# Three matmuls on constant weights ahead of each half's second feed-forward layer, in a one-core hybrid transformer block

## The reference, cut to what matters

```python
x = x + attn_a(layernorm(x))    # 16 heads of 8, softmax over 1024 keys
x = x + ffn(layernorm(x))
x = x + attn_b(layernorm(x))    # 8 heads, the nearest 32 of a window of 64, then a decoder
x = x + ffn(layernorm(x))

def ffn(x):                     # weights are +1 or -1
    h = s0 * (concat([x, -x]) @ w0)     # 256 -> 512
    h = s1 * ((relu(h) * 2) @ w1)       # 512 -> 512: the layer of the change
    return s2 * ((relu(h) * 2) @ w2)    # 512 -> 128
```

## Time and profile before

| | |
|---|---|
| median of three runs (lowest, highest) | 2771.61 us (2760.75, 2773.98) |
| the profiled execution, its own time | 2766.34 us |
| its span, first to last instruction | 2764.6 us |
| mean granted TensorE clock | 0.907 of full speed |
| busy: PE, ACT, DVE, POOL | 86%, 78%, 77%, 20% of the span |
| matmuls of the second layer (hparts,W) | 992 of 1024 under this name, 310.2 us busy |

### The profile page before, as it was taken

One profiled execution on the slowest core, in us unless ns is written; L12 is line 12 of the kernel. 1 busy time (PEld: TensorE's weight loads), 2 busy tenths in 40 slices (PEclk: granted clock), 3 DMA queues, 4 the chain that ended last, 5 costly groups with the idle time before them and its releaser, 6 DMA issues.

```text
span 2764.6 us, 62837 instructions
## 1 busy us (share of the span) xinstructions
PE 2381.7 (86%) x22227; PEld 1037.3 (38%) x22227; DVE 2120.0 (77%) x10307; ACT 2161.5 (78%) x2935; POOL 559.5 (20%) x744
## 2 busy tenths in 40 slices
PE   3788788998899888999899898999899888997766
PEld 1111343344332543335432453335433454235444
DVE  4910769977798778987799777987799877992684
ACT  3799678988699777987789777997779876994443
POOL 3020013212141113211141111412132120111241
PEclk6599698999899998999899998999999998998777
DMA  3111000110011001110001100110001100000000
GB/s 88 37 44 42 11 24 18 52 47 10 24 52 50 19 7 27 57 55 9 24 30 45 47 6 24 58 52 11 19 16 59 52 10 16 12 19 1 19 21 12
DMA packets 98525, 84.92 MB, mean 31 GB/s; under 512 B 19954, under 2 KB 79540, under 8 KB 98212
## 3 DMA queue, kind: packets, MB, share of 16 engines
q1 hardware_dynamic: 97968, 80.41, 9.8%
q10 hardware_dynamic: 244, 0.49, 0.1%
HBM read 55.32 MB, written 25.44 MB: 29 GB/s over the span
## 4 chain that ended last, share of the span: by engine, by line
PE 45%; ACT 31%; DVE 16%; issue 6%; SPq 2%; POOL 1%; DMA 0%; ACTq 0%; DVEq 0%; POOLq 0%
PE banks L909 41%; ACT PT L1268 17%; ACT pq L1255 3%; DVE xn L1623 3%; DVE h L1626 3%; DVE pq L1397 2%; PE banks L916 2%; ACT h L1276 1%; ACT hparts L1275 1%; ACT xn L1208 1%; ACT h L1334 1%; ACT h L1337 1%; ACT h L1176 1%; SPq L621 1%; DVE B L1581 1%
## 5 line engine op out<-in xcount | busy, mean ns | idle before, releaser
L1268 ACT ACTIVATE PT<-banks 128x1024 f32<-128x1024 f32 x1024 | 988.8, 1029 | 46.0 <-PE banks L909 40.8
L1397 DVE CUSTOM_DVE_ANT_0 pq<-pq,banks 128x512 f32<-128x512 f32 x1024 | 650.6, 683 | 138.1 <-ACT pq L1255 134.8
L1255 ACT ACTIVATE pq<-banks 128x1024 f32<-128x1024 f32 x512 | 523.6, 1023 | 241.6 <-PE banks L909 214.3
L909 PE MATMUL banks<-PT,Vg 128*9 128x512 f32 x4096 | 546.5, 607 | 6.3 <-ACT PT L1268 6.2
L909 PE MATMUL banks<-K,Q 48*128 48x512 bf16 x2048 | 372.5, 439 | 104.9 <-ACT pq L1255 52.4
L909 PE MATMUL banks<-Q,K 51*128 51x512 bf16 x2048 | 385.0, 396 | 77.7 <-ACT PT L1268 59.3
L1623 DVE MATCH_REPLACE8 xn<-h,xn 128x96 f32<-128x96 f32 x1536 | 352.0, 241 | 0.0
L909 PE MATMUL banks<-hparts,W 128*128 128x512 f32 x992 | 310.2, 452 | 18.7 <-ACT h L1276 6.2
L909 PEld LDWEIGHTS banks<-Q,K 51*128 51x128 bf16 x2048 | 92.2, 93 | 567.6 <-ACT PT L1268 464.9
L859 POOL TENSOR_TENSOR hparts<-h,hparts 128x512 fp32r<-128x512 f32 x108 | 136.1, 1278 | 657.0 <-ACT h L1276 657.0
L1626 DVE MAX8 h<-xn 128x8 f32<-128x96 f32 x1536 | 262.7, 243 | 0.0
(11 more groups left out here) (227 smaller groups left out, 3253.2 us busy)
## 6 DMA issues: line engine op xcount, KB each, us to landing
Vw<-scratch_v SPq DMA_DIRECT2D x256, 51.0 KB, 1.9
scratch_k<-pq SPq DMA_DIRECT2D x24, 384.0 KB, 3.0
K<-scratch_k SPq DMA_DIRECT2D x126, 72.0 KB
qkf<-in_hidden_states SPq DMA_DIRECT2D x16, 512.0 KB, 4.9
scratch_q<-pq SPq DMA_DIRECT2D x24, 256.0 KB, 2.1
Q<-scratch_q SPq DMA_DIRECT2D x126, 48.0 KB
K<-scratch_k SPq DMA_DIRECT2D x126, 48.0 KB
scratch_v<-Bs SPq DMA_DIRECT2D x8, 544.0 KB, 3.6
```

The source lines that it names most:

```text
L909: return pe.matmul(o, l, r, start=start, stop=stop)
L1255: act.activation(cut(g), ring_pair if work is TURN0 and g % 2 else pair[0], ACT.Relu).then_inc(diff_out.sem, 1)
L1268: act.activation(PT[:, at:at + 2, :], pair[g % ESLOTS], ACT.Exp, scale=1.0 if i % 8 < 4 else -1.0).then_inc(probs.sem, 1)
L1397: dve.tensor_tensor_reduce(r, r, pair[1 + g % 2][:, par, :], 1.0, -3.0e38, ALU.subtract, ALU.max, mred[:, par, i, qt:qt + 1]).then_inc(max ...
```

## The change

On PE alone, in front of the first matmul of every half's second layer, the wait for the ring bank comes first, then three matmuls of 128 x 128 weights and 512 columns are issued into that bank (both operands are parts of the constant W1), and only then the wait for the fourth `fa`'s eviction. Nothing reads what they leave: the layer's own first matmul starts the bank anew. The waits themselves are the same ones, in another order. No other engine's stream is touched.

```diff
+            def busy(bank, times):
+
+                for _ in range(times):
+                    mm(bank[:, 0:HALF], W1[:, 0, 0:P], W1[:, 1, 0:HALF], True, True)
+
...
                         if f == 0:
+                            pe.wait_ge(*R.free(c, k))
                             if o == 0:
+                                busy(R.bank(k), 3)
                                 pe.wait_ge(*R.made(c, k, use["fa", (n, 2)], use["fa", (n, 3)]))
-                            pe.wait_ge(*R.free(c, k))
                         if o == 0:
                             pe.wait_ge(*(low_p if side == "p" else low_q).at(b, FC * (n % 2) + f + 1))
```

## The result

The changed kernel takes 2771.32 us (median of 20 runs, 2764.30 to 2779.11), the kernel before 2765.76 us in the runs beside it (20 runs, 2760.01 to 2777.12). The ratio is 1.0019, with a 95% interval from 1.0010 to 1.0028. That is slower by 5.2 us (0.19%): within the 0.5% that the prediction called "same" and inside its range of 2755 to 2781 us, but clear of zero, where the forecast had gain and costs cancel.

The account below looks back on a forecast made before the run. PE's matmuls were taken to bound the kernel, slowed by half-clock stretches after short idle gaps. -14.3 + 4.2 + 2.8 + 4.5 + 2.9 = +0.1 us on 2766.34; forecast 2767 us, range 2755 to 2781.

Parts of the forecast that it names:

- Half (3): Turns 2 to 7: added matmuls fill 1.04 us of PE idle time, half-clock stretches go; -14.3 us.
- there is nothing to give the loss back: From half (3)'s third layer to the next half (3), the chain was taken as no shorter after a long half (3).
- signs of being wrong: Half-clock stretches remaining at half (3), turns shorter than turn 5's by more than the added matmuls, or new low stretches.
- Half (1): Turns 1 to 7, clock low in all: no gain, added matmuls cost their own time; +4.5 us.
- the trio starts when the layer would have, and merely stands in for it: At half (1), the reason given for expecting no gain from the three added matmuls, within the +4.5 us.
- Half (2): Turns 2 to 7: no PE idle time before the layer, so 0.7 us each goes on the path; +4.2 us.
- half (0): Turns 1 to 7: hidden by 1.18 us idle at full clock, 0.7 us in four low-clock turns; +2.8 us.
- Tail: Six places after the turns: costs at (0), (1), (4) and (5), none at (2) and (3); +2.9 us.
- Rival 1: Half-clock stretches stay at half (3), or move by a few us and take the same; 2781 us, chance 0.15.
- Rival 2: At (0) and (1), 14 places cost 1.3 us each, and half (3)'s half-clock stretches stay; 2792 us, chance 0.08.
- Rival 3: Costs at (2), (0) and (1) hide behind ACT and DVE, only the tail's 2.9 remain; 2755 us, chance 0.13.
- The rule named against the change: Clock drops come from longer PE-idle gaps, so filling 1 us gaps at half (3) saves nothing and only costs stay.

Follow-up runs that it names:

- half3_narrow: Changed kernel with added matmuls only at half (3) of turns 2 to 7, each of 8 columns instead of 512; 0.9997 of the kernel before.
- half3_only: Changed kernel with the three added matmuls only at half (3) of turns 2 to 7; 0.9973 of the kernel before, 7.4 us faster.
- early1: As half3_only, plus three matmuls per turn ahead of the wait of the K,Q pair before half (1)'s layer; 0.9962 of the kernel before.
- tail_only: Changed kernel with added matmuls only at the six places of the tail; 0.9992 of the kernel before.
- not_half3: Changed kernel with added matmuls at the 26 other places, none at half (3) of turns 2 to 7; 1.0059 of the kernel before, 16 us slower.
- early_both: As half3_only, plus three matmuls ahead of each of three waiting K,Q pairs per turn, one before half (1)'s layer, two behind; 0.9916 of the kernel before.
- early_ln: As half3_only, plus three matmuls ahead of each of two K,Q pairs about 22 us behind half (1); 0.9895 of the kernel before, 2738.91 us.
- half3_half1: Changed kernel with added matmuls only at half (3) and half (1), outside the tail; 0.9999 of the kernel before.
- early_narrow: As early_both, but the early added matmuls stream 8 columns instead of 512, those at half (3) whole; 0.9964 of the kernel before.

## Why the prediction was wrong

**Half (3), forecast -14.3.** The mechanism at the place was right: the trio fits the idle 1.04 us, the falls of turns 2, 4, 6 and 7 are gone, that of turn 3 is shorter (and turn 5 has a short one that it had not), and half3_narrow shows that it is the clock. The figure was right for the place (-12.6 in the changed trace, -13.9 in half3_only) and wrong for the kernel: 7.4 us. This is the step that failed, and the term that the sum had wrong: "there is nothing to give the loss back". It was read from the distance between one half (3) and the next, 302.0 and 300.5 us, as if that distance were fixed. The two distances quoted stand behind turns 2 and 5, whose halves (3) are the shortest, so they do not bear on long ones; behind turns 3, 4 and 6 it is 302.2, 303.6 and 300.0 us, not shorter either. But it is not fixed: it contains falls of its own, which come or stay away, and with the trios in place more of them came behind half (1) (24.2 us over the least in half3_only, 10.9 to 22.3 without wide trios). The reading of turn 7 was slightly off, too: 2239.05 - 2221.54 is 17.51 and not 17.44, which leaves the sum as it is. Two of the prediction's own signs of being wrong are in the changed trace: a fall remains at (3) in turn 3, and new ones stand where there were none, as in turn 6 above.

**Half (1), forecast +4.5.** Too small as well. Its seven trios cost 11.6 us alone and 7.2 beside half (3)'s, where the places show 3.6 to 5.8. The sentence "the trio starts when the layer would have, and merely stands in for it" held, and early1 shows what the place is worth: in front of a wait as many matmuls cost nothing.

**Half (2), +4.2, and half (0), +2.8.** The places cost 3.1 and 1.5 in the changed trace; alone the trios cost 6.6 and 5.5 us, with intervals of 4 us to either side. The cover at (0), 1.18 us of idle time, was there and held at full clock.

**Tail, +2.9.** 3.9 in the changed trace, but tail_only gives -2 us with an interval that takes in zero. The costs at (0) and (1) are there; in its trace they are made up for further on.

**The sum.** Two runs split it. Everything but half (3) (not_half3) cost 0.59%, 16 us, against a forecast of 14.4, which lies inside its interval. Half (3) alone gained 0.27%, 7.4 us, against 14.3, which does not. So the miss of the sum is half (3)'s: its whole local gain was taken, and half of that did not reach the end. Added, the two runs give +0.32%, uncertain by 0.17%; the whole change measures +0.19%. Trios outside half (3) may cost less when half (3) is covered (0.46% against 0.59%), but that difference is within the noise. The five places taken alone add up to -0.27 + 0.42 + 0.24 + 0.20 - 0.08 = +0.51%, uncertain by 0.3%, so that the parts don't add is not shown either.

**The rivals.** Rival 1 (falls stay, or move by a few us and take the same) is wrong for the place: the falls there went or got shorter. But about half of the gain was lost again, and the traces have more falls about 50 us behind half (1), which the rival did not name. Rival 2 priced the trios at (0) and (1) at 18.2 us; alone they cost 5.5 + 11.6 = 17.1. That is near by luck: the seven places of each cost 2.8 and 3.6 us by the account, not the 7 x 1.3 = 9.1 of its mechanism, and the rival's other half, that falls stay at (3), did not come. Rival 3 (the costs hide) holds at (0) where the clock is full, and in the tail's sum by tail_only. Its condition, trios in idle time that ACT sets, is what early_both and early_ln then built.

**The rule named against the change.** The section "Why this matters for your kernels" of the Trainium skill's "TensorE: Matmul & The Clock Gate" lays drops to long idle gaps between bursts. Here trios into stretches of 1.04, 0.96 and 0.78 us took falls away: those at (3) alone won 7 us, all of them together 29. By that rule they would have won nothing, and the measurement decides.

**What stays open.** Why half of what half (3) gains is lost again is not known. Falls behind half (1) come with trios at any of the four halves, so a shift in the time of what follows may be the cause as well as the missing falls at (3); no run moved the work without adding matmuls. No trio was tried in the low stretch of 13.7 us at the change from the maxima to the softmax (740.0 to 753.7 in turn 2 of the kernel before, clock 0.50).

## What to carry to other kernels

Filler matmuls paid here in front of a wait that PE had anyway, into a bank that was free before that wait; behind the wait the same filler cost its own time and more (early1 0.9962 against half3_half1 0.9999). Look for all short idle stretches that a fall of the clock follows, not for the one that was noticed first: the early trios behind half (1) brought the time from half3_only's 0.9973 to 0.9916 (early_both) and 0.9895 (early_ln), two to three times what the trio at half (3) had won. And where falls come and go between executions of one kernel, a gain read at one place is not the kernel's: time each place alone, in many runs, before adding them up.

## What was unexpected in the hardware

The clock falls with no idle stretch in front. Before `sq,own` in turn 6 of the changed kernel PE went from one matmul to the next (the rows above, from 2008.72 to 2011.14, have no idle time in them), and stood at half clock from 2011.2 on. In the kernel before the same matmuls, again without idle time, kept the full clock. The 16 `blk,sq` matmuls have 8 columns each. Filler of 8 columns gained nothing either: half3_narrow 0.9997 and early_narrow 0.9964, where 512 columns gave 0.9973 and 0.9916.

A higher mean clock is no sign of a faster kernel when matmuls are added: 0.914 against 0.909 over timed runs, at 5 us more.
